# One attention head of four turned in 32x32 blocks by VectorE and put together by DMAs

## The reference

```python
q, k, v = (proj(Wq), proj(Wk), proj(Wv))              # x @ W.T, heads of 32
scores = jnp.einsum('bhsd,bhtd->bhst', q, k) * scale
scores = jnp.where(mask[None, None, :, :], -jnp.inf, scores)
attn = jax.nn.softmax(scores, axis=-1)
out = jnp.einsum('bhst,bhtd->bhsd', attn, v)
out = out.transpose(0, 2, 1, 3).reshape(B, S, E) @ Wo.T
xn = out / rms * rms_scale * (1.0 + sc[:, None, :]) + shift[:, None, :]
x = x + xn
x = x + hamilton(q_left_n, hamilton(x * spectral_gate, q_right_conj))
```

## Time and profile before

| what | value |
|---|---|
| three runs, median (lowest to highest) | 856.99 us (856.95 to 858.18) |
| span of the profiled execution | 855.4 us |
| PE / DVE / ACT / POOL busy | 846.5 / 628.7 / 615.9 / 482.5 us |
| DMA: bytes, share of the 16 engines | 153.76 MB, 65.8% |
| turns (L788) | 2048 transposes |
| move outs on DVE (L901) and ACT (L1013) | 256 and 256 |
| one whole unit (start of values to start of the next) | 17.8 us |

### The profile page before, as it was taken

The page is one execution under the profiler, slowest core; times in us unless marked ns, Lnnn a source line. Parts: engine busy times, 40 slices in busy tenths (PEclk is TensorE's granted clock), DMA queues, the critical chain, the costliest instruction groups (busy, mean ns, idle before and its releaser), DMA issues.

```text
span 855.4 us, 17179 instructions
## 1 busy us (share of the span) xinstructions
PE 846.5 (99%) x5344; PEld 640.8 (75%) x5344; DVE 628.7 (73%) x1524; ACT 615.9 (72%) x1504; POOL 482.5 (56%) x346
## 2 busy tenths in 40 slices
PE   9999999999999999999999999999999999999997
PEld 6788888888887777767777677776777767777774
DVE  5521321322338899999999999999999999999886
ACT  6232332232329899999999999999999999999882
POOL 0999990000000111666777667776677766777794
PEclk9999999999999999999999999999999999999999
DMA  8854644654599658786687775788668777569201
GB/s 288 339 212 164 233 172 184 220 185 183 182 284 272 138 112 231 173 203 147 149 204 162 157 207 135 156 185 209 143 148 204 164 160 207 131 157 245 68 26 51
DMA packets 82355, 153.76 MB, mean 180 GB/s; under 512 B 8520, under 2 KB 9160, under 8 KB 82272
## 3 DMA queue, kind: packets, MB, share of 16 engines
q1 hardware_dynamic: 82128, 152.49, 65.8%
q10 hardware_dynamic: 144, 0.26, 0.1%
HBM read 102.35 MB, written 50.36 MB: 179 GB/s over the span
## 4 chain that ended last, share of the span: by engine, by line
PE 97%; DVE 1%; issue 1%; ACT 1%; POOL 0%; DVEq 0%; ACTq 0%
PE banks L788 26%; PE banks L120 14%; PE banks L816 13%; PE banks L851 10%; PE banks L471 9%; PE banks L473 9%; PE banks L472 9%; PE banks L797 2%; PE banks L831 1%; PE banks L456 1%; PE banks L444 0%; DVE probs L685 0%; ACT turned_probs L1013 0%; PE banks L510 0%; DVE banks L955 0%
## 5 line engine op out<-in xcount | busy, mean ns | idle before, releaser
L137 ACT ACTIVATE probs<-probs,least 128x512 f32<-128x512 f32 x512 | 363.4, 713 | 0.0
L129 DVE CUSTOM_DVE_ANT_0 probs<-banks,mask_bias 128x512 f32<-128x512 f32 x512 | 330.0, 681 | 37.5 <-PE banks L120 37.5
L788 PE MATMUL banks<-ident,probs 128*128 128x128 f32 x2048 | 306.4, 272 | 0.8 <-DVE turned_probs L901 0.7
L788 PEld LDWEIGHTS banks<-ident,probs 128*128 128x128 f32 x2048 | 252.6, 140 | 56.7 <-ACT probs L137 2.0
L120 PE MATMUL banks<-k_rows,q_rows 128*128 128x512 f32 x496 | 236.2, 478 | 0.0
L901 DVE COPY turned_probs<-banks 128x512 f32<-128x512 f32 x256 | 175.5, 686 | 2.3 <-PE banks L788 2.3
L400 DVE SCALAR_TENSOR_TENSOR late<-banks,late 128x512 fp32r<-128x512 f32 x64 | 43.9, 690 | 158.7 <-ACT late L337 158.7
L1013 ACT ACTIVATE turned_probs<-banks 128x512 f32<-128x512 f32 x256 | 147.1, 587 | 17.0 <-PE banks L788 13.5
L685 POOL TENSOR_TENSOR late<-rot,late 128x2048 f32<-128x2048 f32 x28 | 129.2, 4615 | 0.0
L337 ACT ACTIVATE late<-banks 128x512 fp32r<-128x512 f32 x64 | 38.2, 598 | 119.6 <-PE banks L473 112.5
L816 PE MATMUL banks<-turned_probs,v_sb 128*32 128x512 f32 (+1 forms) x1088 | 117.0, 570 | 1.3 <-ACT turned_probs L1013 1.3
(11 more groups left out here) (134 smaller groups left out, 1263.0 us busy)
## 6 DMA issues: line engine op xcount, KB each, us to landing
q_rows<-q_scratch SPq DMA_DIRECT2D x128, 256.0 KB, 6.1
k_rows<-k_scratch SPq DMA_DIRECT2D x124, 256.0 KB, 6.5
q_scratch<-late SPq DMA_DIRECT2D x64, 256.0 KB, 2.3
k_scratch<-late SPq DMA_DIRECT2D x64, 256.0 KB, 2.3
v_sb<-v_scratch SPq DMA_DIRECT2D x8, 1024.0 KB, 11.4
out<-late SPq DMA_DIRECT2D x29, 256.0 KB, 7.5
raw<-in_xT SPq DMA_DIRECT2D x7, 1024.0 KB, 5.4
v_scratch<-v_out SPq DMA_DIRECT2D x28, 256.0 KB, 2.0
```

The costliest lines, as they stand in the source:

```text
L129: dve.tensor_tensor_reduce(self.probs[:, n % RING, :], self.ps[:, n % SCORE_BANKS, :], self.mask_bias[:, c, :], 1.0, 3e38, ALU.add, ALU.mi ...
L137: act.activation(self.probs[:, n % RING, :], self.probs[:, n % RING, :], ACT.Exp, bias=self.least[:, n % 32:n % 32 + 1], scale=-1.0, accum ...
L788: last = pe.transpose(turn_bank("tile", n)[:, j * P:(j + 1) * P], probs[:, n % RING, j * P:(j + 1) * P], ident[:, :])
```

## The change

In the 30 whole groups the four tiles of the first head (i = 0) are no longer turned by TensorE. They are spread over the group: `ORDER` puts them at places 0, 3, 6 and 9. VectorE transposes each 128x512 tile within its 32x32 blocks, from the ring to a new tensor `blocks`, at places 1, 4, 7 and 9. A block then lies in the right order inside but on the partitions of its own query rows. When the fourth is done, 16 DMAs of 64 KB (32 partitions x 2 KB) on SP's queue bring the blocks to their partitions in `turned_probs`, and the values of the group wait for all of them. In `turned_probs` the first head's columns then stand in another order, so its values matmuls read and write by runs of 32 columns. `BY_ACT` gives ScalarE 8 of the other 12 tiles and VectorE 4.

Besides: the rows of q and k stand on every fourth partition (`r::HG`) and not on 32 neighbouring ones, for q and k alike, so the contraction is the same. To make room `RING` goes from 12 to 10, `scaled` and `junk` lie in `o_T`, with waits for its other users, and the setup's scratch is shortened.

```diff
-RING, SLOTS = 12, HG + 1
+RING, SLOTS = 10, HG + 1
+BLOCK_PLACES = (0, 3, 6, 9)
+BLOCKS_AT = (1, 4, 7, 9)
+def tiles_of_group(chunks):
+    tiles = [(i, c) for i in range(HG) for c in chunks]
+    if chunks == ALL:
+        blocked, tiles = tiles[:TC], tiles[TC:]
+        for place, tile in zip(BLOCK_PLACES, blocked):
+            tiles.insert(place, tile)
+    return tiles
-BY_ACT = {'early': '0101010101010101', 'whole': '0101010101010101', 'half': '01010011'}
+BY_ACT = {'early': '-10-11-10-101101', 'whole': '-10-11-10-101101', 'half': '01010011'}
...
-        sp.dma_start(f32(self.q[r * D:(r + 1) * D, u % 2]),
+        sp.dma_start(f32(self.q[r::HG, u % 2]),
...
-        scaled = sb("scaled", [P, E])
-        junk = sb("junk", [P, E], BF16)
+        scaled, junk = o_T, o_T[:, 0:E // 2].bitcast(BF16)
...
+            def move_blocks(v):
+                sp.wait_ge(blocked, TC * (v + 1))
+                if v >= 2:
+                    sp.wait_ge(valued, v - 1)
+                slot = HG * v % SLOTS
+                for a in (0, 2, 1, 3):
+                    for k in (0, 2, 1, 3):
+                        sp.dma_start(turned_probs[k * D:(k + 1) * D, slot, a, :],
+                                     blocks[a * D:(a + 1) * D, k].rearrange("p j c t -> p (j c t)")).then_inc(moved, 16)
...
+                if chunks == ALL:
+                    move_blocks(v)
                 if u + 2 < U:
                     load_unit(u + 2)
...
+                    to, of = value_ps[i * D:(i + 1) * D, cols], turned_probs[:, (HG * u + i) % SLOTS, part, cols]
+                    if i == 0 and chunks == ALL:
+                        if part == 0:
+                            pe.wait_ge(moved, 16 * TC * TC * (v + 1))
+                        to = to.rearrange("p (c a t) -> p a c t", c=TC, a=TC)
+                        of = turned_probs[:, HG * u % SLOTS, :, part * P:(part + 1) * P].rearrange(
+                            "p a (c t) -> p a c t", c=TC)
+                    last = pe.matmul(to, v_sb[:, b % 2, part, h * D:(h + 1) * D], of,
...
-                turn(n)
+                if BY_ACT[n] != "-":
+                    turn(n)
...
+            def block(n):
+                v, u, i, c = ORDER[n]
+                dve.wait_ge(exped, n + 1)
+                if n == 0:
+                    dve.wait_ge(projected, (TC + 2 * NG) * (B - 1) + 2 * NG)
+                if c == 0 and v > 0:
+                    dve.wait_ge(moved, 16 * TC * TC * v)
+                dve.transpose(blocks[:, :, :, c, :].rearrange("p k j t -> p j k t"),
+                              probs[:, n % RING, :].rearrange("p (j k t) -> p j k t", j=TC, k=TC)).then_inc(blocked, 1)
...
+                if chunks_of(v) == ALL and t in BLOCKS_AT:
+                    block(FIRST[v] + BLOCK_PLACES[BLOCKS_AT.index(t)])
```

More of the change, by code:

```diff
@@ L32 @@
 V = len(GROUPS)
-ORDER = [(v, u, i, c) for v, (u, chunks) in enumerate(GROUPS) for i in range(HG) for c in chunks]
+BLOCK_PLACES = (0, 3, 6, 9)
[7 more added lines that the diff above has]
+    return tiles
+ORDER = [(v, u, i, c) for v, (u, chunks) in enumerate(GROUPS) for i, c in tiles_of_group(chunks)]
 SIZE = [HG * len(chunks) for _, chunks in GROUPS]
@@ L105, in __init__ @@
         self.least = ctx.enter_context(nc.sbuf_tensor("least", [P, 32], F32))
-        self.scored, self.masked, self.exped, self.turned, self.inverted, self.spread, self.passed = [
+        self.scored, self.masked, self.exped, self.turned, self.blocked, self.inverted, self.spread, self.passed = [
             ctx.enter_context(nc.semaphore(n))
-            for n in ("scored", "masked", "exped", "turned", "inverted", "spread", "passed")]
+            for n in ("scored", "masked", "exped", "turned", "blocked", "inverted", "spread", "passed")]
     def score(self, pe, n):
@@ L125, in mask @@
         dve.wait_ge(self.scored, n + 1)
-        if n >= RING:
-            dve.wait_ge(self.turned, n - RING + 1)
+        if n >= RING and BY_ACT[n - RING] == "-":
+            dve.wait_ge(self.blocked, n - RING + 1 - TURNS[n - RING + 1])
+        elif n >= RING:
+            dve.wait_ge(self.turned, TURNS[n - RING + 1])
         dve.sem_inc(self.passed, 1)
@@ L689, in attention @@
         rows.last_k = values_and_k[:, 0]
-        late_mix = [probs[:, 4 * j:4 * j + 4, :] for j in range(3)]
+        late_mix = [probs[:, 4 * j:4 * j + 4, :] for j in range(2)] + [blocks[:, :, :, :, :].rearrange(
+            "p k j c t -> p k (j c t)")]
+        late_junk = probs[:, RING - 1, 0:E // 2].bitcast(BF16)
         late_out = [turned_probs[:, 3, j, :] for j in range(3)]
@@ L923, in held_out @@
                     dve.wait_ge(held_stored, 16 * c)
-                dve.tensor_copy(scaled[:, :], y_ps).then_inc(held_copied, 1)
+                else:
+                    dve.wait_ge(qk_stored[0], 16 * 4 * B)
+                dve.tensor_copy(held_v, y_ps).then_inc(held_copied, 1)
             def rescale(m):
@@ L1072, in _ @@
                     split_hi(v - 1)
[L1073 removed]
+                if n > 0 and by_act(n - 1):
                     move_out(n - 1)
```

46 lines of the change are left out of this document (27 added, 19 removed).

## The result

The changed kernel takes 1106.07 us (median of 4 runs, 1104.85 to 1107.58), the kernel before 856.97: a ratio of 1.29, 95% interval 1.288 to 1.292. The direction is as forecast, the size is not: +249 us instead of +99, above the end of the range at 1040. Rival 5, in which TensorE's clock falls in the wait, gave 1064 and is still too low.

The account below looks back on a forecast made before the run. TensorE, busy 99%, bounds the kernel at 17.8 us per unit. Fourth block at 11.96 plus handover 9.1 makes 21.1 us, +3.3 x 30 = +99, so 956 us; range 880 to 1040.

Parts of the forecast that it names:

- Rival 5: TensorE's clock falls to half in its wait before the values: +3.6 us per unit, 1064 us; chance 0.11.
- the handover: From the fourth block's end to the next values: SP issues 16 DMAs, they land, TensorE sees it; 9.1 us, 5.86 available.
- TensorE's and VectorE's savings: Per unit, 1.4 us less TensorE turning and 1.06 us of VectorE before mask 8; both were to count nothing.
- the rows stay hidden: Row loads queued on SP behind the 16 moves would still arrive before score 16 reads them, by 3 to 4 us.
- the pitch of an issue: On SP's queue, the first move takes 0.37 us to issue and each further one 0.475, whatever its bytes.
- Landing: A move from SBUF to SBUF lands 2.0 us after issue, as stores from SBUF on an idle queue do.
- the upper bound of 13.2 us: The handover's upper bound, with moves landing after 6.1 us like the row loads, as if the queue were full.
- The place of the fourth block: On VectorE, 12 operations of 0.607 us from mask 8 on; the fourth block ends 11.96 us behind the values' start.
- rival 4: VectorE's block transposes take twice a copy instead of the 0.61 us assumed: +1.8 us per unit, 1010 us; chance 0.1.
- rival 2: The moves are just in time and DMA volume binds: 18.0 us per unit, 863 us or no change; chance 0.04.
- Ring, `o_T`, strided values: Ring of 10: nothing; scaled and junk in `o_T`: nothing or 0.1 us; values in 32-column runs: at most 0.9 us per unit.
- The port rule: 32 neighbouring partitions reach 8 of 16 DMA ports, 218 GB/s; spread rows reach all 16 and load faster, sum unchanged.

Follow-up runs that it names:

- eight moves of 128 KB: The changed kernel with the same 1 MB per unit moved in 8 DMAs of 128 KB instead of 16 of 64 KB: 907.07 us, ratio 1.057.
- the idle matmuls: The changed kernel with 24 thrown-away bf16 matmuls of 512 columns put on TensorE ahead of its wait for the moves: 1052.83 us, ratio 1.228.
- moves from HBM: The changed kernel with its 16 moves reading from the q scratch in HBM instead of the blocks in SBUF: 1014.9 us, one execution.
- the kernel of two queues: The changed kernel with blocked tiles at places 0, 2, 4, 6, transposes at 1, 1, 2, 2, and 4 of 16 moves on ScalarE's queue: 879.63 us, ratio 1.026.
- blocks when ready: The changed kernel with blocked tiles at places 0, 2, 4, 6 and their transposes at 1, 1, 2, 2: 911.35 us, ratio 1.066.
- blocks when ready, rows together: Blocked tiles at places 0, 2, 4, 6, transposes at 1, 1, 2, 2, q and k rows back on 32 neighbouring partitions: 913.41 us.

## Why the prediction was right and wrong

- **The mechanism was right.** The values wait for the moves in every whole unit (30 times), the gate is the fourth block plus the handover, TensorE's and VectorE's savings vanish in that wait, and the rows stay hidden.
- **The step that failed first: the pitch of an issue.** The term 0.37 + 14 x 0.475 + 2.0 took the price of loads from HBM for copies from SBUF. Landing (2.0 us) and the start of SP (0.03 us behind the block) were right; 16 issues took 10.1 to 10.7 us, 0.63 to 0.67 each. The last starts 0.6 us before their end, so 9.5 to 10.1, 2.0 to land and 0.1 make 11.6 to 12.2 us; 11.67 and 12.24 were seen. With 11.9 instead of 9.1 the handover costs 2.8 us more per unit, 84 us. The stated argument, that the pitch doesn't go with bytes, holds (eight moves of 128 KB), but its evidence didn't: the 0.43 us of the 1 MB load is that of the row loads ahead of it. What the pitch goes with is source and pattern, and the upper bound of 13.2 us was built from a slower landing, with no bound above 0.475 for the pitch itself. The range then stopped at 1040, short of its own bound: 11.96 + 13.2 = 25.2 us per unit would have made about 1077.
- **The step that failed second: rival 5 was made an alternative.** The forecast itself contained a stand of 3.5 us, so the clock was a term of its sum. The page of the Trainium skill that was weighed there (TensorE: Matmul & The Clock Gate, What's actually happening) says that an idle engine falls back to half its clock; the windows agree, with 0.50 at the end of a stand of 5.9 us, and the first head's values at 1.2 GHz. The rows before had no such wait, which is no evidence against it. The size of the rival was too large: +3.6 us for values wholly at 1.2 GHz. They had 2.4 GHz again before their end, so they took 5.8 us in the mean, and the idle matmuls gave 1.8 us per unit back. That this step fails by itself is shown by the moves from HBM, which have the forecast's pitch and wait: values of 5.24 instead of 3.64 us are 48 us in 30 units, 11 more lie outside the units, and 956 becomes the 1015 measured.
- **The place of the fourth block was right.** It stands 13.62 us behind the values, forecast 11.96; 1.55 of the difference are the slower values of this unit; the count of 12 operations held.
- **The sum made anew:** 11.96 + 2.15 (values of 5.8 instead of 3.64) + 11.9 = 26.0 us per unit, measured 25.91. Left of the 250 us are 6.8 before the first values and 8.7 behind the last. In front of the first values stands the same wait, of 6.67 us; of the 8.7, 2.4 us are the last slow values and some 3 a wait of TensorE for a copy of VectorE in the half units, 0.74 us before:

```profile
1069.22 1.09 PE L825 MATMUL banks<-ident,probs 128*128 128x128 f32 x4 [3.87 <-DVE turned_probs L955]
```

The trace leads on from there. The copy stands behind the residual of VectorE, which waited 3.91 us (0.77 before) for GpSimd; GpSimd had stood 14.52 us (2.39 before) without the x of its chunk. SP issued that load at 1035.63, behind the moves and the rows and 3.2 us behind the last whole unit's values; before, it went out 1.2 us ahead of them. No run tests this, but the kernel of two queues has the same wait (3.77 us) with no slow values. The other 3 us of the 8.7 stay open.
- **Transposes** (rival 4): 0.61 us from start to start, a copy's price, as taken. **DMA volume** (rival 2): 183 GB/s and a share of 0.60 in the unit, so not the bound. **Ring, `o_T`, strided values**: nothing seen; the last is shown by the 3.64 us of the experiments at full clock.
- **The port rule** of the Trainium skill (SBUF — State Buffer, Door 1: The DMA port swizzle) agrees with the trace in direction: 266 to 301 GB/s while rows load, against 227 before, and a landing of 4.3 us against 6.1. The 227 lie 4% above the 218 that the page gives for 8 ports. It brought no time, as forecast, where nobody waits for rows.

## What to carry to other kernels

A small DMA is paid for on the queue that issues it: count the issues between the last producer and the waiting engine, take the price from rows with the same source and pattern, and leave the bytes for later. Where a forecast makes TensorE stand still for some microseconds, put the slower start of what follows into the sum itself and not among the rivals. To take 1.4 us from an engine that was busy 99% gains nothing until every wait that comes next, down to one mask behind two transposes, is taken away as well.

## What the runs showed of the hardware

- In a run of like ones, a DMA over 32 partitions occupied SP's queue for 0.43 us (median) from HBM to neighbouring partitions (256 KB), 0.42 from HBM for a move of 64 KB, 0.60 from HBM to every fourth partition, and 0.59 (0.63 to 0.67 from start to start) from SBUF to SBUF, with 64 or 128 KB alike. On ScalarE's queue the same move took 0.53 us at the median, 0.51 to 1.58.
- A DMA right behind such a run showed the run's duration and not one of its own: the load of v 0.43 us behind row loads of 0.43, and 0.59 behind row loads of 0.60.
- A move of 64 KB within SBUF landed 2.0 us after its issue where no row loads were under way, and after 2.7 to 2.9 at the median in the two kernels that have row loads to neighbouring partitions beside it.
- The length of a wait alone doesn't tell what clock follows. The values took 3.64 us behind waits of 1.1 us, and 4.92 to 6.58 behind waits of 5.9, at whose end the grant was 1.2 GHz. They also took 3.64 us behind a wait of 2.71 (blocks when ready) and of 3.20 (moves from HBM), but 5.34 behind one of 2.27 (blocks when ready, rows together), where the grant fell from 1.00 to 0.53 only while they ran.
- VectorE transposed 128x512 f32 in 32x32 blocks in the time of a copy, 0.61 us from start to start.
